# Running the value matmuls of two key blocks as one group every second step of an attention stage, on one Trainium2 core

## The reference

```
scores = jnp.einsum('bhqd,bhkd->bhqk', qh, k_rec) / math.sqrt(d)
decay = jnp.exp(-LAMBDA_DECAY * jnp.abs(t[:, None] - t[None, :]))
scores = scores * decay[None, None, :, :]
attn = jax.nn.softmax(scores, axis=-1)
out = jnp.einsum('bhqk,bhkd->bhqd', attn, v_rec)
```

## Time and profile before

| | |
|---|---|
| time, median of 3 runs | 2783.0 us (2781.36 to 2785.18) |
| span of the profiled execution | 2775.7 us |
| what lies around the span (median less span) | 7.3 us |
| PE busy | 2597.7 us, 94% of the span |
| DVE busy | 2345.5 us, 85% |
| ACT busy | 1601.3 us, 58% |
| POOL busy | 970.2 us, 35% |

### The profile page before, as it was taken

The page is one execution under the profiler, slowest core; times in us unless marked ns, Lnnn a source line. Parts: engine busy times, 40 slices in busy tenths (PEclk is TensorE's granted clock), DMA queues, the critical chain, the costliest instruction groups (busy, mean ns, idle before and its releaser), DMA issues. The chain is left out here.

```text
span 2775.7 us, 54634 instructions
## 1 busy us (share of the span) xinstructions
PE 2597.7 (94%) x15110; PEld 1209.7 (44%) x15110; DVE 2345.5 (85%) x4659; ACT 1601.3 (58%) x2988; POOL 970.2 (35%) x865
## 2 busy tenths in 40 slices
PE   5887679999999999999999999999978999999998
PEld 3333213343444444344344344443323566666665
DVE  5888698888888888888888888888756999999997
ACT  3666507777777777777777777777762222222221
POOL 3666522122122122122122122122231555555654
PEclk8767659999999999999999999999997999999999
DMA  4777864446455455455456455456201111111110
GB/s 152 246 247 255 265 129 73 71 74 99 62 85 87 63 82 82 71 78 86 70 78 86 72 80 86 69 79 94 39 11 38 37 41 40 40 40 42 40 32 18
DMA packets 207121, 238.56 MB, mean 86 GB/s; under 512 B 32256, under 2 KB 150784, under 8 KB 206720
## 3 DMA queue, kind: packets, MB, share of 16 engines
q1 hardware_dynamic: 194560, 218.56, 40.7%
q0 software_dynamic: 3072, 8.39, 1.2%
q10 hardware_dynamic: 9216, 8.39, 0.9%
HBM read 149.79 MB, written 83.89 MB: 84 GB/s over the span
## 5 line engine op out<-in xcount | busy, mean ns | idle before, releaser
L856 DVE CUSTOM_DVE_ANT_0 unread<-max_ps,toeplitz_sb 128x1024 bf16<-128x1024 f32 x1024 | 1219.2, 1219 | 230.5 <-PE max_ps L689 221.9
L817 ACT ACTIVATE probs<-score_ps 128x512 f32<-128x512 f32 x2048 | 1113.3, 597 | 438.3 <-PE score_ps L722 299.7
L689 PE MATMUL max_ps<-k_low,q_low 96*128 96x512 bf16 x2048 | 717.5, 393 | 30.0 <-DVE ident_bf L847 17.9
L651 POOL TENSOR_TENSOR probs<-probs,up_probs 128x512 f32<-128x512 f32 x256 | 336.8, 1316 | 624.4 <-ACT up_probs L821 624.4
L750 PE MATMUL pv_ps<-probs,v 128*32 128x512 f32 x4096 | 548.9, 608 | 3.4 <-POOL probs L651 3.4
L722 PE MATMUL score_ps<-q_low,k_low 99*128 99x512 bf16 (+3 forms) x1280 | 407.9, 320 | 4.9 <-ACT probs L817 4.1
L714 PE MATMUL score_ps<-q_up,k_up 99*128 99x512 bf16 (+3 forms) x1280 | 408.0, 319 | 4.5 <-ACT probs L817 3.8
L1284 PE MATMUL gu_ps<-wgu_t,turned 128*128 128x512 f32 (+1 forms) x768 | 314.7, 559 | 0.6 <-DVE hid L1445 0.6
L657 POOL DMA_DIRECT2D attn<-out_n x64 | 48.8, 762 | 698.3 <-DVE out_n L920 674.8
L714 PEld LDWEIGHTS score_ps<-q_up,k_up 99*128 99x128 bf16 x1280 | 123.8, 97 | 350.4 <-ACT probs L817 325.2
L689 PEld LDWEIGHTS max_ps<-k_low,q_low 96*128 96x128 bf16 x2048 | 194.0, 99 | 156.5 <-DVE row_max L856 83.9
(11 more groups left out here) (145 smaller groups left out, 3218.2 us busy)
## 6 DMA issues: line engine op xcount, KB each, us to landing
splits<-parts SPq DMA_DIRECT2D x128, 384.0 KB, 2.6
q_low<-splits SPq DMA_DIRECT2D x192, 128.0 KB, 4.4
k_low<-splits SPq DMA_DIRECT2D x192, 128.0 KB, 7.0
q_up<-splits SPq DMA_DIRECT2D x192, 128.0 KB, 9.4
k_up<-splits SPq DMA_DIRECT2D x192, 128.0 KB, 12.0
v_padded<-v_out SPq DMA_DIRECT2D x64, 256.0 KB, 3.5
v<-v_padded SPq DMA_DIRECT2D x32, 512.0 KB, 13.9
x_in<-in_L_attn_x SPq DMA_DIRECT2D x16, 512.0 KB, 4.6
```

The source lines that it names most:

```text
L651: nc.gpsimd.tensor_tensor(probs[:, g % PROBS, :, at:at + P], probs[:, g % PROBS, :, at:at + P], up_probs[:, g % 2], ALU.add).then_inc(diag ...
L689: mm = pe.matmul(max_ps[:, i % 2, half * HALF:(half + 1) * HALF], low[0][u][0:KROWS, h, qb * P:(qb + 1) * P], low[1][u][0:KROWS, h, half * ...
L817: nc.scalar.activation(probs[:, g % PROBS, h, :], score_ps[:, i % 2, :], ACT.Exp).then_inc(exp_done, 1)
L856: nc.vector.tensor_tensor_reduce(unread[:, i % 2, :], max_ps[:, i % 2, :], toeplitz[:, at:at + S], 1.0, -3.0e38, ALU.mult, ALU.max, row_ma ...
```

## The change

After the scores and maxima of each step TensorE ran the values of the step two back. Now it runs no values after an even step, and after an odd step g the values of steps g - 3 and g - 2, one group behind the other. Nothing else is changed. The prologue skips the values of the first two steps as before, and after the last step the values of the last two steps follow as before.

```diff
@@ -774,7 +774,8 @@
                             max_tile(ahead[0], ahead[1], ahead[2] + j // 2, j % 2)
                     if h == 1 and is_diagonal(g):
                         up_diagonals(b, u, g)
-                if not (first and g < LAG):
+                if g % 2 == 1 and not (first and g < LAG):
+                    values(*steps_back(b, u, g, LAG + 1))
                     values(*steps_back(b, u, g, LAG))
                 if g == 5 and not first:
                     turn_out(2 * unit - 1)
```

## The result

The changed kernel takes 2950.0 us (median of 4 runs, 2944.0 to 2954.5) against 2782.2 us. The ratio is 1.061, 95% interval 1.059 to 1.063: it is slower by 168 us. The prediction was 2991 us with a range of 2930 to 3035, slower with a chance of 0.95. The profiled execution of the changed kernel has a span of 2951.2 us and a time of 2953.0, so 1.8 us lie around the span.

What follows compares the result with a forecast made beforehand. Plain steps were held by a loop of waits through ScalarE and the values, diagonal ones by TensorE. VectorE-held pairs and small operations add 6.68 us per unit, 208 in all: 2991 us, range 2930 to 3035.

Steps and rivals of the forecast that it cites:

- the loop through ScalarE and the values: Plain step before the change: waits from first score through exponentials, fourth score and values add up to 2.88 us.
- Plain and diagonal pairs: Two steps together: values start at 4.59 us (plain) and 5.46 (diagonal), making pairs 0.78 and 0.79 us longer.
- the odd step's first scores early: Odd step of a plain pair: TensorE gets through its first scores early, as there were no values before.
- The doubled group: Two value groups in a row on TensorE: taken as 1.95 us, between 1.90 and 2.10.
- one of the signs of being wrong that I had named: Changed kernel's profile: the forecast would be wrong if the two value groups took clearly less than 1.9 us.
- the small operations: VectorE's reciprocal of step 6 and splitting pieces of step 8 now lie in the loop: +0.4 us per unit.
- the last two units: End of the stage: 4 pairs with maxima add 3.1 us and 12 without add 5 us.
- L762 in step 10: Turning of the output on TensorE: regains some 0.07 us by standing in a step with room.
- Around the span: Time outside the profiled span: 7.3 us, which is how the median of 2783.0 stands to the span.
- ScalarE alone: Rival: ScalarE sets the pair; plain pair +0.16 us, diagonal about the same, 2796 us; chance 0.03.
- The faster rival: TensorE's own time decides: 0.15 us saved per pair over 256 pairs, 38 us, giving 2745 us; chance 0.04.
- The clock: Rival: TensorE's clock falls to 1.2 GHz in a tenth of the pairs, about 3125 us; chance 0.05.

Runs made afterwards that it cites:

- e6: Kernel before, with VectorE's row maximum over 512 instead of 1024 columns of each tile and exponentials scaled by 0.01: 2761.4 us, ratio 0.994.
- e10: Kernel before, with VectorE's row maximum over 512 of 1024 columns and ScalarE's exponential over 256 of 512: 2737.4 us, ratio 0.985.
- e5: Changed kernel, with VectorE's row maximum over 512 instead of 1024 columns of each tile and exponentials scaled by 0.01: 2818.4 us, ratio 1.014.
- e7: Changed kernel, with three quarters of the value matmuls narrowed to half their columns and exponentials scaled: 2795.7 us (one run).
- e2: Changed kernel, with L734 moved behind the third score and the last half of the maxima in odd diagonal steps: 2902.4 us, ratio 1.044.
- e9: Changed kernel, with VectorE's row maximum over 512 of 1024 columns and ScalarE's exponential over 256 of 512: 2736.6 us, ratio 0.985.
- e1: Changed kernel, with the third half of the maxima moved behind the third score in odd steps: 2968.3 us, ratio 1.067.

## Why the prediction was right, and where it was off

- **What bounds each step.** That plain steps of the kernel before are held by the loop through ScalarE and the values holds: e6 leaves them at 2.88 us, e10 brings them to 2.84. TensorE's own work was only 0.04 us behind. Diagonal steps don't move in either, they are TensorE's own.
- **Plain and diagonal pairs.** The values start at 4.60 us in steps 4 and 5 and at 5.47 in the diagonal pairs, as worked out. e5, e7 and e2 show the cause as stated: VectorE's two tiles in the even step, and its limiting operation, release TensorE late in the odd step. In most pairs VectorE decides by 0.3 to 0.7 us. In steps 4 and 5, the very pair whose 4.60 fits the working, it decides by 0.14 only (6.46 against 6.32 in e5), because I left ScalarE's exponential of the last diagonal block out. Nor does TensorE get through the odd step's first scores early, as I wrote: the first of them waits 0.61 us for ScalarE. VectorE's wait ends last even so. VectorE was idle for 1.5 us in steps 4 and 5 and for 1.4 in the diagonal pair shown; over the eight pairs of that unit it was 1.05 to 2.63, a wider spread than the predicted 1.4 to 1.9.
- **The doubled group** is the largest term that was off: 1.86 us where I took 1.95, below my lower bound of 1.90 and so, by the letter, one of the signs of being wrong that I had named. It makes the loss smaller and leaves its cause as it is.
- **The sum.** The growth of the span was 175.5 us instead of 208. A unit in the middle of a batch grew by 5.80 us instead of 6.68, 26 us over 30 units: about 0.75 us a unit by the doubled groups, 0.08 by the small operations (0.32 us instead of 0.40), and the rest because two steps before are some hundredths longer than I took them. The stalls at the batches came to 25 us instead of 28. The start of the stage, the first batch (whose units grew by 5.2 to 5.7 us) and the last two units, for which I had 8 us, add nothing together. Against these, 4 us lie ahead of the attention stage (the first maximum starts at 353.5 instead of 349.1 us), which the change doesn't touch.
- **L762 in step 10** doesn't stand in a step with room, as I wrote. It waits for VectorE's copy in each of the 30 units:

```profile
PE side_ps L762 <- DVE max_turned L882: 22.9, 30, 0.8
```

- **Around the span** I put 7.3 us, from the median of other runs. The changed kernel has 1.8, which is 5.5 us less. The last 3 of the 41 us are that its profiled execution (2953.0) lies above the median (2950.0). All the larger misses point the same way, and so the time is at the lower edge of the mechanism's own range of 2950 to 3030.
- **The rivals.** ScalarE alone is the next limit. That e5 has the very 5.92 us that I gave for it is luck: the values start at 4.06 instead of 3.97 us, and the shorter doubled group makes up for it. The faster rival would need customers that take scores at TensorE's pace; e9 shows that even with both halved, it comes out level. The clock stayed at 0.99, with TensorE busy for 91% of the stage and 89% of the span, where I expected about 87%.

No version tried beats the kernel before with the full work done. e6, e9 and e10 are ahead of it by 0.6 to 1.5%, and all three leave out work.

## What to carry to other kernels

Here an engine that feeds two others was away from both for longer than their buffers last, and the time that it saved by being away less often didn't come back: the others couldn't work ahead, and in the step that was meant to catch up their own speed was the limit. Before grouping work, count what each consumer has in its banks at the moment the group starts (here two exponentials, 1.1 us, and two tiles, 2.3 us, less what it is behind) and follow one period by hand through all queues; a working of that kind gave the start of the values within 0.01 us for the pairs shown. List every operation of each engine in the period, though: one exponential left out of the list is why steps 4 and 5 gained nothing in e1. And see what is queued behind each wait on an engine that works in order: moving four small matmuls (L734) behind the third score and the last half of the maxima was worth 48 us.

## What the runs showed of the hardware

- Two groups of four f32 matmuls on the four column quarters (128 x 32 weights, 512 columns) take 1.86 us to the next score, one takes 1.00. The second costs only 0.86. Inside the doubled group the second half of a group and the next group start 0.43 to 0.45 us after what stands before them, so the 0.10 us ahead of a group are paid once.
- Halving the columns doesn't halve an operation: the exponential from PSUM took 597 ns for 512 columns and 383 for 256 (e10), the product with row maximum 1217 ns for 1024 (changed kernel) and 687 for 512 (e5).
